# LoRA-A inside the last gate and up tile of a two-layer adapted transformer block, with another order of loads and splits at the start

## The reference, cut to what matters

```python
def lora_add(base, inp, A, B):
    Ab = A[layer_idx][lora_indices]
    Bb = B[layer_idx][lora_indices]
    t = jnp.einsum('bri,bni->bnr', Ab, inp)
    return base + jnp.einsum('bor,bnr->bno', Bb, t) * SCALE
gate = lora_add(jnp.einsum('bnh,fh->bnf', x, W_gate), x, A_gate, B_gate)
up = lora_add(jnp.einsum('bnh,fh->bnf', x, W_up), x, A_up, B_up)
act = jax.nn.silu(gate) * up
down = lora_add(jnp.einsum('bnf,hf->bnh', act, W_down), act, A_down, B_down)
```

## Time and profile before

| | |
|---|---|
| time before, median of 3 runs | 360.72 us (360.45 to 361.3) |
| the profiled execution | 359.89 us |
| its span, first to last instruction | 358.2 us |
| PE busy | 354.3 us, 1728 matmuls |
| DVE, ACT, POOL busy | 197.6, 141.2, 83.2 us |
| moved by DMA | 38.86 MB, mean 108 GB/s |

### The profile page before, as it was taken

One profiled execution on the slowest core, in us unless ns is written; L12 is line 12 of the kernel. 1 busy time (PEld: TensorE's weight loads), 2 busy tenths in 40 slices (PEclk: granted clock), 3 DMA queues, 4 the chain that ended last, 5 costly groups with the idle time before them and its releaser, 6 DMA issues.

```text
span 358.2 us, 4760 instructions
## 1 busy us (share of the span) xinstructions
PE 354.3 (99%) x1728; PEld 299.2 (84%) x1728; DVE 197.6 (55%) x303; ACT 141.2 (39%) x191; POOL 83.2 (23%) x89
## 2 busy tenths in 40 slices
PE   8999999999999999999999999999999999999996
PEld 7888888888888888988888898888888888888886
DVE  3758664245434533576574476769888868511101
ACT  5567444234423432434662552547363353201100
POOL 1738886644240001100000000000032054002200
PEclk9999999999999999999999999999999999999999
DMA  7855542333130041579317209201042012101011
GB/s 253 274 167 168 176 133 62 113 102 88 53 108 0 0 171 47 164 276 345 96 48 214 93 2 354 116 5 53 3 158 77 2 59 73 47 29 59 31 59 59
DMA packets 14979, 38.86 MB, mean 108 GB/s; under 512 B 2305, under 2 KB 4097, under 8 KB 13681
## 3 DMA queue, kind: packets, MB, share of 16 engines
q1 hardware_dynamic: 11728, 31.24, 25.8%
q0 software_dynamic: 2656, 6.95, 6.6%
q10 hardware_dynamic: 576, 0.43, 0.4%
HBM read 36.51 MB, written 2.10 MB: 108 GB/s over the span
## 4 chain that ended last, share of the span: by engine, by line
PE 99%; DVE 0%; issue 0%
PE ps L1052 28%; PE ps L1053 28%; PE ps L1054 28%; PE ps L1174 3%; PE ps L1072 3%; PE ps L1080 1%; PE ps L1087 1%; PE ps L1103 1%; PE ps L1091 1%; PE ps L1095 1%; PE ps L1264 1%; PE ps L1251 1%; PE ps L1273 0%; PE ps L1282 0%; DVE x L1045 0%; DVE warm L746 0%
## 5 line engine op out<-in xcount | busy, mean ns | idle before, releaser
L1052 PE MATMUL ps<-x_hl,w_hl 128*128 128x512 f32 x160 | 62.8, 392 | 0.0
L1053 PE MATMUL ps<-x_hl,w_hl 128*128 128x512 f32 x160 | 62.7, 392 | 0.0
L1054 PE MATMUL ps<-x_hl,w_hl 128*128 128x512 f32 x160 | 62.3, 389 | 0.0
L383 POOL DMA_INDIRECT b_raw<-b_gu,row_of x36 | 36.1, 1003 | 34.7 <-DVE b_st L713 25.4
L421 POOL TENSOR_TENSOR am_hl<-am_raw,am_hl 128x512 fp32r<-128x512 f32 x8 | 11.1, 1392 | 136.8 <-ACT am_hl L438 136.8
L734 DVE TENSOR_TENSOR glu<-glu,ps 128x512 f32<-128x512 f32 x22 | 15.0, 685 | 37.6 <-PE ps L1072 37.6
L1054 PEld LDWEIGHTS ps<-x_hl,w_hl 128*128 128x128 f32 x160 | 30.1, 188 | 6.5
L438 ACT ACTIVATE act<-glu 128x512 f32 (+1 forms) x22 | 13.8, 632 | 54.3 <-DVE glu L734 54.2
L1052 PEld LDWEIGHTS ps<-x_hl,w_hl 128*128 128x128 f32 x160 | 30.1, 188 | 5.2
L1053 PEld LDWEIGHTS ps<-x_hl,w_hl 128*128 128x128 f32 x160 | 30.2, 189 | 4.8
L1053 PE MATMUL ps<-act,wd_hl 128*128 128x512 f32 x80 | 31.1, 389 | 0.0
(11 more groups left out here) (139 smaller groups left out, 700.6 us busy)
## 6 DMA issues: line engine op xcount, KB each, us to landing
wc_raw<-mask_w SPq DMA_DIRECT2D x8, 1024.0 KB, 7.4
w_raw<-w_gu SPq DMA_DIRECT2D x9, 512.0 KB, 3.4
wd_raw<-w_dn SPq DMA_DIRECT2D x10, 256.0 KB, 3.0
x_raw<-x_t SPq DMA_DIRECT2D x8, 256.0 KB, 5.3
w_raw<-w_t SPq DMA_DIRECT2D x2, 1024.0 KB, 6.9
x<-x_t SPq DMA_DIRECT2D x2, 1024.0 KB, 6.1
am_raw<-a_moe SPq DMA_DIRECT2D x8, 256.0 KB, 2.7
bm_raw<-b_moe SPq DMA_DIRECT2D x4, 512.0 KB, 3.8
```

The source lines that it names most:

```text
L383: nc.gpsimd.indirect_dma_start(b_raw[f % 2][:, p].rearrange("q m f -> q (m f)"), None, b_gu, bass.IndirectOffsetOnAxis(ap=row_of[:, f - 2, ...
L1052: nc.tensor.matmul(out, w_high, m_high, start=start, stop=False)
L1053: nc.tensor.matmul(out, w_high, m_low, start=False, stop=False)
L1054: return nc.tensor.matmul(out, w_low, m_high, start=False, stop=stop)
```

## The change

- LoRA-A moves into the last tile. The stationary operand of tile 10 (`w_last`) is made once for each pair of sequences: 96 columns of weights, high and low, and in the 32 free columns that pair's LoRA-A ranks, gate's in the gate operand, up's in the up operand. The tile's matmuls then have 256 columns (a pair) in place of 512, and their output rows 96 to 127 are LoRA-A's result, which DVE masks from there. `lora_down` is gone.
- Tile 10 is therefore computed early, in two halves (`project_last(s)`): after the first half of tiles 0 and 1, and after the first three LoRA-B groups. The PE loop runs over tiles 2 to 9. `FIRST_EVICTED` gives the order of the first six evictions and `FIRST_BANK` their PSUM banks.
- Both products of the gate and up adapters now stand in one 32-row group, so t's split and LoRA-B's low rows need one row block instead of two, of twice the length, and LoRA-B's stationary operand has 96 rows. The first LoRA-B load has the rows of tiles 0, 1 and 10 (`b_three`) and comes in two groups of two pairs.
- Loads: x's first chunk of 512 tokens becomes two of 256, each with a semaphore, split and projected by itself (`project_pair`); tile 1's first weight piece goes from ACT's to SP's queue; tile 10's weights and two adapters come before x's second half; POOL loads two adapters, two LoRA-B groups, two adapters, waits for x's last chunk and loads the other two groups. The constants' mask comes alone, before the last two adapters. POOL's load of the down projection's adapters waits until tile 10 is computed, since `w_last` lies where they go.
- Ten warm-up matmuls become seven. The down projection's LoRA-A takes the tiles in the order of their eviction.

```diff
-WARM_UP = 10
+WARM_UP = 7
+LAST = FT - 1
+FIRST_EVICTED = ((0, 0), (1, 0), (LAST, 0), (LAST, 1), (0, 1), (1, 1))
+FIRST_BANK = (4, 0, 2, 4, 6, 0)
...
         def _(sp):
-            load_x0(0)
+            for h in range(2):
+                sp.dma_start(x_raw[:, 0, h * PAIR:h * PAIR + PAIR],
+                             x_t[:, 0, h * PAIR:h * PAIR + PAIR]).then_inc(dma_x0_pair[h], 16)
+            sp.dma_start(w_raw[1][:, 0], w_gu[1, :, 0]).then_inc(dma_w_first[1][0], 16)
             load_x0(1)
...
+            sp.dma_start(w_last_raw[:], w_gu[LAST]).then_inc(dma_w_last, 16)
+            sp.wait_ge(dma_small, 16)
+            for b in range(2):
+                load_a(b, dma_a[0])
             for k in range(KD):
                 sp.dma_start(x_raw[:, k, HALF:T], x_t[:, k, HALF:T]).then_inc(dma_x1[k], 16)
-            for b in range(A_BY_SP):
...
+            for b in range(4, 6):
+                load_a(b, dma_a[1])
...
         def _(pool):
+            load_a(0)
...
-            load_b_first()
+            load_b_first(0)
+            load_a(1)
+            pool.wait_ge(dma_x1[KD - 1], 16)
+            load_b_first(1)
...
                 if f == AD_LOADS_AFTER:
+                    pool.wait_ge(up_ready, evicted(LAST, 1) + 1)
                     load_ad()
...
         def _(act_e):
+            for p in range(2):
+                w_last_high(p)
+            a_high(0)
+            for k in range(KD):
                 x_high(k, 1)
...
-            for u in range(2):
-                b_first_high(u)
+            b_first_high(0)
+            for p in range(2, NPAIR):
+                w_last_high(p)
+            a_high(1)
             t_high(0)
+            first_silu(0)
+            first_silu(1)
+            first_act_high(0)
+            first_act_high(1)
+            first_silu(2)
+            first_act_high(2)
+            b_first_high(1)
             w_high(2, 0, 2)
...
             t_high(1)
+            first_silu(3)
             b_high(2, 0, 2)
...
         def _(dve):
+            b_first_low(0)
+            w_last_low(2, 5)
...
             t_mask(0)
+            w_last_low(3, 6)
             t_low(0)
+            a_low(1, 7)
+            first_gate(0)
+            first_gate(1)
+            first_act_low(0)
+            first_act_low(1)
+            first_gate(2)
+            first_act_low(2)
             b_first_low(1)
             w_low(2, 0)
             t_mask(1)
             t_low(1)
...
         def _(pe):
-            def lora_down(p):
...
+            def project_last(s):
+                bank = FIRST_BANK[2 + s]
+                pe.wait_ge(wl_hi, 4 * s + 4)
+                pe.wait_ge(wl_lo, 4 * s + 4)
+                for m in range(2):
+                    if s == 1:
+                        pe.wait_ge(glu_done if m else silu_done, 1)
+                    for p in (2 * s, 2 * s + 1):
+                        cols = slice(p * PAIR, p * PAIR + PAIR)
+                        for k in range(KD):
+                            last = mm3(ps[:, bank + m, PAIR * (p % 2):PAIR * (p % 2) + PAIR],
+                                       w_last[:, p, 0, k, m], w_last[:, p, 1, k, m],
+                                       x_hl[:, 0, k, cols], x_hl[:, 1, k, cols],
+                                       k == 0 and p % 2 == 0, k == KD - 1 and p % 2 == 1)
                 last.then_inc(t_ready, 1)
...
+            for h in range(2):
+                project_pair(h)
+            project_first(1, 0)
+            for k in range(1, KD):
                 for u in range(2):
                     project_first(u, k)
-            pe.wait_ge(a_hi, 4)
-            pe.wait_ge(a_lo, 4)
-            for p in range(2):
-                lora_down(p)
+            project_last(0)
...
-            for p in range(2, NPAIR):
-                lora_down(p)
-            adapt_first(0)
+            pe.wait_ge(t_hi, 2)
+            pe.wait_ge(t_lo, 1)
+            pe.wait_ge(bf_hi, 3)
+            pe.wait_ge(bf_lo, 3)
+            for n in range(3):
+                adapt_first(n)
+            project_last(1)
             for m in range(2):
-                pe.wait_ge(t_masked, m + 1)
-                project(1, 1, m, 1)
-            adapt_first(1)
+                pe.wait_ge(glu_done if m else silu_done, 2)
+                project(1, FIRST_BANK[5] + m, 1)
+            pe.wait_ge(t_hi, 4)
+            pe.wait_ge(t_lo, 2)
+            pe.wait_ge(bf_hi, 6)
+            pe.wait_ge(bf_lo, 6)
+            for n in range(3, 6):
+                adapt_first(n)
```

More of the change, by code:

```diff
@@ L115, in slots @@
         def slots(name, shape, dtype, offset):
-            return [at(f"{name}{u}", shape, dtype, R_U + 20 * KB * u + offset) for u in range(2)]
+            return [at(f"{name}{u}", shape, dtype, R_U + 20 * KB * (1 - u) + offset) for u in range(2)]
         x_hl = at("x_hl", [P, 2, KD, T], F32R, R_X)
@@ L753, in _ @@
             nc.vector.tensor_copy(w_hl[0][:, 0, 0:1], w_raw[0][:, 0:1]).then_inc(w_hi, 1)
-            for k in range(2):
-                x_low(k, 0)
-                for u in range(2):
-                    w_first_low(u, slice(k, k + 1), 2 * k + u + 1)
+            for h in range(2):
+                pair = slice(h * PAIR, h * PAIR + PAIR)
+                dve.wait_ge(x_hi if h else x_pair_hi, 1)
+                low(x_hl[:, 1, 0, pair], x_raw[:, 0, pair], x_hl[:, 0, 0, pair]).then_inc(x_lo if h else x_pair_lo, 1)
+                w_first_low(h, slice(0, 1), h + 1)
+            x_low(1, 0)
+            for u in range(2):
+                w_first_low(u, slice(1, 2), 3 + u)
             x_low(2, 0)
@@ new lines, in a_low, with b_first_low @@
+            def a_low(g, n):
+                for par in range(2):
+                    dve.wait_ge(wl_hi, n + par)
+                    low(a_part(1, g, par), a_own(g, par), a_part(0, g, par)).then_inc(wl_lo, 1)
+            for p in range(2):
+                w_last_low(p, p + 1)
+            a_low(0, 3)
+            for k in range(KD):
+                x_low(k, 1)
+            def b_first_low(g):
+                two, rows = slice(2 * g, 2 * g + 2), slice(64, 96)
+                for u, stack in enumerate((b_other, b_st[1], b_st[0])):
+                    dve.wait_ge(bf_hi, 3 * g + u + 1)
+                    low(stack[rows, two], b_first[rows, two, u], stack[rows, two]).then_inc(bf_lo, 1)
@@ L801, in _ @@
             b_low(2, 0)
-            gate(3, 1, 7)
-            for u in range(2):
-                act_low(2 + u, u, u, 1)
-            with dve.Fori(0, (FT - 3) // 2) as i:
+            first_act_low(3)
+            first_gate(4)
+            first_act_low(4)
+            first_gate(5)
+            first_act_low(5)
+            with dve.Fori(0, (FT - 5) // 2) as i:
                 for u in range(2):
@@ L1057, in halves, with project @@
                 return slice(s * HALF, s * HALF + HALF)
-            def project(slot, bank, m, s, first=False, part=range(KD)):
+            def project(slot, bank, s, first=False, part=range(KD)):
                 for k in part:
@@ L1094, in project_first @@
                 for m in range(2):
[L1095 removed]
+                    nc.tensor.matmul(ps[:, FIRST_BANK[u] + m], w_hl[u][:, 1, k, m], x_hl[:, 0, k, halves(0)],
                                      start=False, stop=False)
[L1098 to L1106 removed]
@@ new lines, in adapt_first, with project_pair, pass_of @@
+            def adapt_first(n):
+                f, s = FIRST_EVICTED[n]
+                for m in range(2):
+                    if f == LAST:
+                        adapt(b_st[0], FIRST_BANK[n] + m, s, F_LAST)
+                    else:
+                        adapt(b_st[1] if f else b_other, FIRST_BANK[n] + m, s)
+            def project_pair(h):
+                pair = slice(h * PAIR, h * PAIR + PAIR)
+                def pass_of(part_w, part_x):
+                    for m in range(2):
+                        nc.tensor.matmul(ps[:, FIRST_BANK[0] + m, pair], w_hl[0][:, part_w, 0, m], x_hl[:, part_x, 0, pair],
+                                         start=h == part_w == part_x == 0, stop=False)
+                pe.wait_ge(w_hi, 1)
+                pe.wait_ge(x_hi if h else x_pair_hi, 1)
+                pass_of(0, 0)
+                pe.wait_ge(x_lo if h else x_pair_lo, 1)
+                pass_of(0, 1)
+                pe.wait_ge(w_lo, 1)
+                pass_of(1, 0)
```

334 lines of the change are left out of this document (173 added, 161 removed).

## The result

The changed kernel takes **356.71 us** (median of 4 executions, 356.29 to 356.91) where the kernel before, measured with it, takes 360.64: a ratio of **0.9884, interval 0.9868 to 0.99**. Two later comparisons (runs 5 and 10) gave 0.9871 (0.9854 to 0.9889) and 0.9878 (0.986 to 0.9896). Forecast were 356.9 us and "faster"; both hold, the second by far more than the 0.2% that the prediction took as what a measurement can tell. The profiled execution took 356.68 us, its span is 355.0.

A forecast was written before the change was run, and what follows sets the result against it. PE, busy 354.3 of 358.2 us, was taken as the bound. -3.82 + 0.52 + 0.07 - 0.65 + 0.10 = -3.8 us took the profiled 359.89 to 356.1; adding 0.83 gave 356.9, range 355.8 to 358.9.

The forecast's parts named there:

- LoRA-A goes: PE: the 32 LoRA-A matmuls, 1.91 us per 16, disappear into the last tile's free output rows: -3.82 us.
- rival E: Last tile: its free columns aren't free, a half costs as much as a whole matmul: 367.2 us; chance 0.01.
- The start: First k-step of tiles 0 and 1: first real matmul at 4.75, step over at 7.85 instead of 8.51: -0.65 us.
- Rival B: Slow clock: first k-step of both tiles may run at half speed, ending at 10.15; 359.2 us; chance 0.07.
- No wait: Tile 1's first k-step at 6.5: its weight piece, now on SP's queue, is there when PE wants it.
- Loads: Weights and two adapters ahead of x's second half take 1.6 us; last tile's splits done at 14.2, worst 15.8: 0.
- rival C: Stall ahead of t: first LoRA-B rows land at 20, not 17, t split 1.6 us late; 358.5 us; chance 0.10.
- The second half of the last tile: ACT and DVE must finish the second t within PE's 12.67 us, the thinnest cover: +0.1 us, bounds 0 and 1.0.
- Nothing else: Tiles 2 to 9 are as before; the down projection's adapters load at about 40 us, needed at 140: no cost.
- From the profiled execution to the median: Last step: 0.83 us, the earlier profiled execution's distance below its median 360.72, added to 356.1, giving 356.9.
- A: The start gives nothing, as both first loads share the DMA engines: -3.1, 357.6 us; chance 0.14.
- D: Slower than before: second adapter group, ahead of t's highs on ACT, lands after 27.7; 361.6 us; chance 0.04.

The follow-up runs named there:

- run 5: The changed kernel again, unedited: 356.82 us (356.02 to 357.72), ratio 0.9871.
- run 10: The changed kernel a third time, unedited, beside two variants on the same chip: 356.85 us, ratio 0.9878.
- run 7: The kernel before with LoRA-B on 96 of 128 rows, leaving out t's low part for the up adapters: one execution, 361.78 us.
- run 9: The kernel before again, unedited, for a second profile: 361.22 us.
- run 2: The changed kernel with the old start (ten warm-ups, x's first chunk whole, tile 1's first weight piece on ACT's queue): 357.40 us, ratio 0.9897.
- run 3: The changed kernel with ten warm-up matmuls instead of seven, nothing else: 356.82 us, ratio 0.9888.
- run 4: The changed kernel with DVE's second mask of t ahead of tile 2's weight lows: 356.29 us, ratio 0.987.
- run 12: The changed kernel with DVE's second mask of t ahead of tile 2's weight lows and LoRA-B on 128 rows, 32 of them zero: 355.95 us, ratio 0.9851.
- run 1: The kernel before with the new start alone (seven warm-ups, x's first chunk in two pieces, tile 1's weight piece on SP's queue): 365.43 us, ratio 1.0077.
- run 6: The kernel before with the new start, and SP's adapters issued and split ahead of x's second half: 361.34 us, ratio 1.0004.

## Why the prediction was right

**LoRA-A goes: exact.** -3.82 us, and the last tile's halves took 5.76 instead of 5.75. The free columns of the stationary operand cost nothing that these rows show, so rival E falls. Each split added 0.012 us, as the down projection's row had it; the Trainium skill's 2.5 ns for a matmul's fixed cost ("TensorE: Matmul & The Clock Gate", section "Wait — 56ns, not 53.3ns?") is not what these matmuls show, each of which has a weight load of its own (1744 of either).

**The start: right in kind, too large against the first profile, of the right size against the others.** The first real matmul came at 4.25, earlier than the 4.75 taken and than the bound of 4.4, but that step's "some 0.3 more while the array is slow" was too little. All twelve halves but the last were slow in the first profile and cost 2.60 us, where 1.44 + 0.3 had been taken. The second k-step stood at 8.24, 7.81 and 7.92 in three profiles of the changed kernel, against 7.85 forecast: gains of 0.27, 0.70 and 0.59 on the 8.51 of the earlier trace rows. But 8.51 is the earliest of the four traces with the old start; the others have 8.76 (run 7, whose first matmul came 0.34 later), 9.01 (run 9) and 9.12 (run 2), both of which met the slow pace in it. Mean against mean, 8.85 and 7.99, the start gains 0.86. (The sum of the prediction also counts the +0.07 for x's two pieces twice: it stands in the 1.44 already.)

Rival B had the cause, not the extent: the slow pace ended with the halves, and tile 1's matmuls went 0.23 apart. "No wait" for tile 1's first piece held in the first profile because PE was slow: in run 10 the halves are through at 6.26, ACT has the piece at 6.38, and PE goes on at 6.43. That the point where the clock rises differs from run to run is what the Trainium skill says in "TensorE: Matmul & The Clock Gate" (Part 1, the HAM clock gate); these traces agree, since the distance of two halves falls from 0.21 to some 0.12 us at 6.7, 5.2 and 5.4 us in the three profiles, which all start between 4.20 and 4.25. The number of warm-ups changed nothing in the time (run 3).

**Loads: nothing lost in the first profile, but with less cover than thought.** The last tile's splits were done at 15.85, not 14.2, just after the worst case of 15.8, with 0.56 us to spare; the 1.6 us for the loads ahead of x's second half are those of the weights alone, and with the two adapters of 64 KB they would be 2.1. The first LoRA-B rows were copied at 19.16, not 17, close to rival C's 20; ACT was through with them in time for t's mask, and 1.25 us stayed spare where 1.4 was forecast. The thin place was another: run 5 lost 1.2 us and run 3 0.15 at tile 1's later weights, which the prediction had not looked at.

**The second half of the last tile: right.** +0.18 against +0.1, from the place named; run 4 takes it away. The step of 0.41 us there is one of the signs that the prediction gave for being wrong ("PE starts more than 0.3 apart at 16, 27 or 40 us"), but its own +0.1 on a pitch of 0.23 would have met that sign as well.

**"Nothing else": wrong by 0.2.** The prediction took the loop's tiles as unchanged, but LoRA-B on 96 rows costs more than on 128, not as much or less (runs 7 and 12).

**From the profiled execution to the median: the step that made up for the rest.** Against 359.89 the sum was to be -3.8 and came out as -3.2: the start 0.4 short, the loop 0.2, the stall 0.1; the loop began at 41.93, where 41.5 was forecast. The forecast then added 0.83, the distance of the profiled execution before from its median, as if it held for both kernels. It doesn't: the changed kernel's profile lies at its median (356.68 and 356.71). Run 9 shows what the first profile of before lacked, 0.8 for the pause at tile 2 and 0.5 for the slow first k-step; run 7, with the same order of work, has the pause too (1.19 us of idle PE at the same place), and so have runs 1 and 6 (0.38 and 0.59). None of the profiles of the changed kernel and its variants has it. So the medians gain 3.9 to 4.7 us in the three comparisons where the first pair of traces gains 3.2, and the forecast of -3.8 came near by two errors that cancel, which is luck. That most executions of before have the pause follows from its medians and is not shown one by one.

Why the changed kernel doesn't have the pause is shown in part. In the first profile of before the low part of tile 2's LoRA-B rows is done at 34.52 + 1.39 = 35.91 and PE wants it at 36.15, so 0.24 us are spare; in the changed kernel the row of DVE is

```profile
42.58 1.22 DVE L777 TENSOR_TENSOR b_st<-b_raw,b_st 32x1024 fp32r<-32x1024 f32 x1 [0.26 <-ACT b_st L478]
```

and PE wants it at 44.68, so 0.88 are spare: twelve LoRA-B matmuls stand behind the release of ACT's Silu where there were eight, and the low part is one block instead of two. A release as late as that of run 9 (1.40 - 0.49 = 0.91) would about fit in. It doesn't come, either: ACT's Silu starts 0.49 to 0.55 us after the group in all nine profiles of the changed kernel and its variants, and 1.01, 1.07 and 1.40 after it in runs 7, 6 and 9. Why the release is late only in the old order stays open; no run separates it.

**The rivals.** A (the start gives nothing) falls by run 2, but is what the old order would have had (run 6). D's kind of loss, a late load that PE meets, came at other places: in run 1 at the adapters (2.5 us), and in the changed kernel at tile 1's weights (run 5, 1.2 us).

## What to carry to other kernels

Where PE is the whole chain, count the moving columns it streams: here the work that fits into unused columns of a stationary operand was free, and every added matmul and every odd operand shape had a price to be read from a like row. An earlier start is worth something only if each later in-order wait has room for it, so follow PE to the next two waits, since a pause moves there and may cost the clock as well. Before a sum is made against one profiled execution, ask what its distance to the median is made of, because the change may remove just that; here a second trace of the unchanged kernel would have told.

## What was not expected of the hardware

- A pause of 2.5 us on PE was followed by 3.3 us at the lower clock: the column shows 0.51, 16 matmuls took 3.28 us instead of 1.91 (run 1). At the start of the kernel the same column prints 1.00 over halves that are 0.217 us apart; there only the distance of starts shows the level.
- Two LoRA-B matmuls on 96 rows cost 0.0065 us more than on 128, between matmuls on 128 rows (95.33 us for the loop in all eight traces with 96 rows, 95.13 in all six with 128; taking rows away from the kernel before and giving them to the changed one both show it).
- The release of ACT by the same PE group came 0.49 us after its start in one execution and 1.40 in another of the same kernel (run 9), with all PE starts around it as they should be. In run 1 the mask of t on DVE waits 3.58 us, until 33.54, for PE's last LoRA-A matmul, which by the trace ended at 29.46. The cause is open.
